# A four-layer cross-attention kernel: two single-precision products split in 16 bit parts, bias products on separate rows of the array, one shift and one exponential per GQA item, and a new order of the work

## The reference

```python
# GQA layer: 16 query heads of width 8, 4 key/value heads, no mask
xn = x * rsqrt(mean(x*x, -1) + 1e-5) * norm_w
q, k, v = xn @ wq, ctx @ wk, ctx @ wv
x = x + softmax(q k^T / sqrt(8)) v @ wo

# MHA layer: 16 heads of width 64
q, k, v = x @ Wq, ctx @ Wk, ctx @ Wv
logits = q k^T / 8 + col_bias        # -20*(1-mask[t]) in up to four key columns
x = x + softmax(logits) v @ Wo + bo
```

## Time and profile before

| | |
|---|---|
| median of three runs | 1851.74 us |
| profiled execution, its own time | 1852.7 us |
| its span, first to last instruction | 1850.9 us |
| PE / DVE / ACT / POOL busy, share of the span | 97% / 86% / 80% / 81% |
| mean granted TensorE clock | 0.977 of full speed |
| DMA | 320.36 MB, mean 173 GB/s |

### The profile page before, as it was taken

The page is one execution under the profiler, slowest core; times in us unless marked ns, Lnnn a source line. Parts: engine busy times, 40 slices in busy tenths (PEclk is TensorE's granted clock), DMA queues, the critical chain, the costliest instruction groups (busy, mean ns, idle before and its releaser), DMA issues.

```text
span 1850.9 us, 72762 instructions
## 1 busy us (share of the span) xinstructions
PE 1792.3 (97%) x28272; PEld 1557.7 (84%) x28272; DVE 1593.3 (86%) x3130; ACT 1471.6 (80%) x2859; POOL 1507.8 (81%) x1880
## 2 busy tenths in 40 slices
PE   6699999999999999999999999999999999999995
PEld 6578888888888888888888888888888888888884
DVE  6589988889888998898888998889888988889973
ACT  4378888888888888888888888888888888888872
POOL 3388888888888888888888888888888888888873
PEclk7599999999999999999999999999999999999998
DMA  5279999999999899999999999999899999989995
GB/s 170 42 140 183 167 187 183 184 182 166 178 192 180 181 168 184 185 173 188 175 180 187 177 175 178 182 190 177 176 178 186 185 173 177 169 176 178 177 165 128
DMA packets 1168210, 320.36 MB, mean 173 GB/s; under 512 B 1140246, under 2 KB 1164124, under 8 KB 1167868
## 3 DMA queue, kind: packets, MB, share of 16 engines
q1 hardware_dynamic: 1167868, 315.69, 93.1%
HBM read 15.93 MB, written 4.19 MB: 11 GB/s over the span
## 4 chain that ended last, share of the span: by engine, by line
PE 92%; issue 1%; DMA 0%; DVE 0%; POOL 0%; SPq 0%; ACT 0%
PE ring L1215 48%; PE sc L1352 11%; PE o_ps L1215 9%; PE o_ps L1370 5%; PE ring L1424 5%; PE sc L1335 4%; PE sc L1350 4%; PE ring L1286 2%; PE ring L1410 1%; PE ring L1405 1%; PE ring L1421 1%; PE sc L1327 1%; PE ring L1263 0%; PE o_ps L1366 0%; PE ring L1266 0%
## 5 line engine op out<-in xcount | busy, mean ns | idle before, releaser
L1215 PE MATMUL ring<-ctx_four,m_w 128*128 128x154 f16 x6144 | 441.4, 230 | 1.5 <-DVE v_tile L915 0.9
L1215 PEld LDWEIGHTS ring<-ctx_four,m_w 128*128 128x128 f16 x6144 | 422.8, 96 | 1.9 <-DVE v_tile L915 1.1
L636 POOL TENSOR_TENSOR p_sg<-arena,p_sg 128x512 f16<-128x512 f32 (+1 forms) x256 | 347.4, 1357 | 89.8 <-ACT p_sg L702 89.8
L1092 DVE TENSOR_TENSOR arena<-sc,row_max 128x616 f32<-128x616 f32 (+2 forms) x512 | 402.6, 797 | 13.2
L641 POOL TENSOR_TENSOR p_sm<-arena,p_sm 128x616 f16<-128x616 f32 x256 | 334.1, 1319 | 4.4 <-ACT p_sm L702 2.5
L664 POOL TENSOR_TENSOR arena<-arena 128x1024 f16<-128x1024 f32 x128 | 273.4, 2136 | 40.5 <-ACT arena L702 40.4
L702 ACT ACTIVATE arena<-ring 128x462 f16<-128x462 f32 (+1 forms) x384 | 198.3, 516 | 133.8 <-PE ring L1215 132.5
L1215 PE MATMUL ring<-wv_m,ctx_four 128*103 128x512 f16 (+1 forms) x1152 | 281.2, 380 | 0.6 <-DVE q_mix L919 0.6
L1071 DVE TENSOR_TENSOR arena<-ring,arena 128x462 f16<-128x462 f32 (+1 forms) x384 | 223.8, 584 | 64.2 <-ACT arena L702 55.4
L1352 PE MATMUL sc<-arena,x_s 128*128 128x512 f16 (+1 forms) x1152 | 262.2, 336 | 0.0
L1089 DVE TENSOR_REDUCE row_max<-sc 128x6 f32<-128x462 f32 (+2 forms) x384 | 223.7, 583 | 44.2 <-PE sc L1352 38.8
(11 more groups left out here) (165 smaller groups left out, 3797.4 us busy)
## 6 DMA issues: line engine op xcount, KB each, us to landing
v_fourth<-v_tile SPq DMA_DIRECT2D x64, 105.6 KB
ctx_nat<-in_ctx_dram SPq DMA_DIRECT2D x64, 77.0 KB
x_nat<-in_x_dram SPq DMA_DIRECT2D x64, 64.0 KB, 2.4
arena<-p_sg SPq DMA_TRANSPOSE x256, 3.9
arena<-p_sm SPq DMA_TRANSPOSE x256, 4.1
out_dram<-y_out SPq DMA_DIRECT2D x64, 64.0 KB, 2.1
v_fourth<-v_tile SPq DMA_DIRECT2D x32, 101.6 KB
arena<-in_L_xattn_Wk_dram SPq DMA_DIRECT2D x2, 1024.0 KB, 6.1
```

What stands on the lines that cost most here:

```text
L636: pool.tensor_tensor(p_sg[k][:, LO, 0:e - a], probs_flat[:, a:e], p_sg[k][:, HI, 0:e - a], ALU.subtract).then_inc(sems["pg_lo"], 1)
L1092: dve.tensor_tensor(shifted[:, hs, :], s_view[:, hs, :], row_max[:, hs].unsqueeze(2).to_broadcast([P, hs.stop - hs.start, S]), ALU.subtrac ...
L1215: ins = pe.matmul(out, a, b, start=(n == 0), stop=(n == len(passes) - 1))
```

## The change

- **Sum of squares.** POOL still squares `x` in f32 (`x_sq`, now two buffers). A new ACT step `squares` writes the square's high part in f16 straight from `x_f`, POOL subtracts it, and `scores_g` uses two f16 passes of one column against `ones_h`.
- **GQA output product.** `wo_g` is f16 high and low; `turned` makes two ACT copies (f16 high, f32), a new POOL step `low_turned` makes the low part, `output_g` has three f16 passes.
- **Bias products.** The six rows of `bias_l` and `bias_r` are copied to partitions 32 to 37 and 64 to 69 as well. `scores_m(m, 0)` issues the three bias products of all three banks at once, each with 6 rows from another group of 32 partitions, and waits for all of the shift before.
- **GQA shift and exponential** are one instruction each (1232 columns). GQA and MHA items have their own `shifted` and `probs` buffers, and the waits go to the item two before of the same kind.
- **Order.** On PE, `rest_and_turn` and the transpose stand at the start of the next pair, `output_m` comes behind the first folded chunk, `values_g` and `turn_inputs` go behind the scores of `m`, `output_g` stands between the first two `scores_m`. The whole lists of a pair are now:
  - PE: `rest_and_turn(g-4)`, `scores_g(g)`, folded 0, `output_m(m-6)`, folded 1 and 2, `keys_values(g+2)`, `scores_m(m,0)`, `output_g(g-4)`, `scores_m(m,1)`, `pick_values(g)`, `turn_inputs(g+4)`, `values_g(g-2)`, `queries(g+2)`, `scores_m(m,2)`, context values, `values_m(m-2)`, context values.
  - DVE: `maximum_g`, folded 0, `finish_m(m-6)`, `shift_g`, folded 1 and 2, `keys_values(g+2)`, `finish_g(g-4)`, `maximum_m` 0 and 1, `shift_m` 0, `normalise_g(g-2)`, `maximum_m` 2, `turn_context`, `shift_m` 1, `queries`, values, `normalise_m(m-2)` 0 and 1, values.
  - ACT: `turned(g-4)`, folded 0, `high_out(m-4)`, `last_layer(m-6)`, folded 1 and 2, `keys_values`, `exponential_g`, `high_g` 0 and 1, `first_x`, `picked_values`, `turn_context`, `queries`, `exponential_m` 0, values, `squares(g+4)`, `high_m` 0, `exponential_m` 1, values, `high_m` 1, `normalise_rest(m-2)`.
  - POOL: `pack_values(g-2)`, `inverse_norm(g)`, `low_turned(g-4)`, `low_out(m-4)`, `spread_keys(g+2)`, `x_parts(m+2)`, `low_part(g)` 0 and 1, `x_parts(g+4)`, `low_part(m)` 0 and 1.
- **Buffers.** The ring's order follows that of PE. `y_out` has four buffers for eight streams, with one more wait on ACT.

```diff
@@ ring_uses
-        return [("ym", m - 6, 0), ("g", lead, chunks[0]), ("g", lead, chunks[1]), ("g", lead, chunks[2]), ("kv", g + 2, 0),
-                *[("ct", g + 4, 0)] * (layer(g + 4) == 0 or n % PAIRS == CT_EXTRA), ("vp", g, 0), ("q", g + 2, 0), *[("v", j, k) for j, k in value_chunks(n)[0:1]], ("yg", g - 4, 0),
-                *[("v", j, k) for j, k in value_chunks(n)[1:2]], ("ot", g - 2, 0)]
+        return [("ot", g - 4, 0), ("g", lead, chunks[0]), ("ym", m - 6, 0), ("g", lead, chunks[1]), ("g", lead, chunks[2]),
+                ("kv", g + 2, 0), ("yg", g - 4, 0), ("vp", g, 0), *[("ct", g + 4, 0)] * (layer(g + 4) == 0 or n % PAIRS == CT_EXTRA), ("q", g + 2, 0),
+                *[("v", j, k) for j, k in value_chunks(n)[0:1]], *[("v", j, k) for j, k in value_chunks(n)[1:2]]]
@@ buffers
-        probs = in_arena(HS, F32).rearrange("p (h s) -> p h s", s=S)
-        shifted = in_arena(HS, F32).rearrange("p (h s) -> p h s", s=S)
+        probs_g, shifted_g = in_arena(HS, F32), in_arena(HS, F32)
+        probs_m, shifted_m = [in_arena(HS, F32).rearrange("p (h s) -> p h s", s=S) for n in range(2)]
@@ SP pair
-                if exists(it, m - 2) and part(m - 2) != 3:
-                    move_values(it, m - 2)
                 if exists(it, g):
                     turn_g(it, g, 0)
                     turn_g(it, g, 1)
+                if exists(it, m) and part(m) != 3:
+                    move_values(it, m)
@@ POOL x_parts, GQA items
-                    pool.tensor_tensor(x_sq[st][:, :], x_f[st][:, :], x_f[st][:, :], ALU.mult).then_inc(sems["sq"], 1)
+                    pool.tensor_tensor(sq[:, :], x_f[st][:, :], x_f[st][:, :], ALU.mult).then_inc(sems["sq_f32"], 1)
+                    pool.wait_ge(sems["sq_hi"], at("sq_hi", it, j, 1))
+                    pool.wait_ge(sems["sq_f32"], at("sq_f32", it, j, 1))
+                    pool.tensor_tensor(x_sp[st][:, LO, :], sq[:, :], x_sp[st][:, HI, :], ALU.subtract).then_inc(sems["sq"], 1)
@@ POOL
+            def low_turned(it, g):
+                pool.wait_ge(sems["ot_copy"], at("ot_copy", it, g, 1))
+                pool.tensor_tensor(o_tg[:, LO, :], o_tf[:, :], o_tg[:, HI, :], ALU.subtract).then_inc(sems["ot_lo"], 1)
@@ ACT
+            def squares(it, g):
+                st = stream(g)
+                act.wait_ge(sems["xg_f32"], at("xg_f32", it, g, 1))
+                act.activation(x_sp[st][:, HI, :], x_f[st][:, :], ACT.Square, scale=1.0).then_inc(sems["sq_hi"], 1)
...
+                act.activation(probs_g, shifted_g, ACT.Exp, bias=log_w[:, :], scale=rstd[:, r:r + 1]).then_inc(sems["pg_exp"], 1)
...
-                high(o_tg[:, :], ring[:, b, 0:T], 1.0).then_inc(sems["ot_copy"], 1)
+                high(o_tg[:, HI, :], ring[:, b, 0:T], 1.0).then_inc(sems["ot_hi"], 1)
+                high(o_tf[:, :], ring[:, b, 0:T], 1.0).then_inc(sems["ot_copy"], 1)
@@ DVE bias_factors, split_gqa_weights
+                for k in range(1, 3):
+                    step(dve.tensor_copy(bias_l[32 * k:32 * k + 6, :], bias_l[0:6, :]))
+                    for n in range(2):
+                        step(dve.tensor_copy(bias_r[n][32 * k:32 * k + 6, :, :], bias_r[n][0:6, :, :]))
+                    low(wo_g[n][:, LO], st_go[:, n, :], W_V, wo_g[n][:, HI]).then_inc(dve_ready, 1)
@@ DVE
-            def shift_g(it, g, k):
+            def shift_g(it, g):
                 dve.wait_ge(sems["sg_max"], at("sg_max", it, g, 1))
-                shifted_free(it, g, k)
-                shift(G_SUB[k], sems["sg_sub"])
+                if exists(it, g - 2):
+                    dve.wait_ge(sems["pg_exp"], at("pg_exp", it, g - 2, 1))
+                shift(shifted_g.rearrange("p (h s) -> p h s", s=S), slice(0, H), sems["sg_sub"])
@@ PE scores_g
-                pe.matmul(sc_flat[:, SS_COL:SS_COL + 1], x_sq[st][:, :], ones[:, :], start=True, stop=True)
+                for i in (HI, LO):
+                    pe.matmul(sc_flat[:, SS_COL:SS_COL + 1], x_sp[st][:, i, :], ones_h[:, :], start=(i == HI), stop=(i == LO))
@@ PE scores_m
-                scores_free(it, m, min(k, 1) + 1)
-                ind = bias_r[w][:, :, :].rearrange("p h s -> p (h s)")
                 a, e = k * BANK, min(HS, (k + 1) * BANK)
-                pe.matmul(sc_flat[:, a:e], bias_l[:, :], ind[:, a:e], start=True, stop=False)
+                if k == 0:
+                    scores_free(it, m, 2)
+                    ind = bias_r[w][:, :, :].rearrange("p h s -> p (h s)")
+                    for b in range(3):
+                        c0, c1, rows = b * BANK, min(HS, (b + 1) * BANK), slice(32 * b, 32 * b + 6)
+                        pe.matmul(sc_flat[:, c0:c1], bias_l[rows, :], ind[rows, c0:c1], start=True, stop=False)
@@ PE output_g
-                pe.matmul(ring[:, b, 0:T], wo_g[w][:, :], o_tg[:, :], start=True, stop=True).then_inc(sems["yg_raw"], 1)
+                split_product(ring[:, b, 0:T], [(hl(lambda i: wo_g[w][:, i, :]), hl(lambda i: o_tg[:, i, :]))]).then_inc(sems["yg_raw"], 1)
@@ PE pair
+                if exists(it, g - 4) or exists(it, m - 4):
+                    rest_and_turn(it, n, g - 4)
                 if exists(it, g):
                     scores_g(it, g)
```

More of the change, by code:

```diff
@@ L796, in queries, with exponential_g @@
                 high(q_hi[:, :, :], ring[:, b, :].rearrange("p (r t) -> p r t", t=T), 1.0).then_inc(sems["q_hi"], 1)
[L798 to L813, removed]
+            def exponential_g(it, g):
+                r = g // 2 % 2
+                act.wait_ge(sems["rstd"], at("rstd", it, g, 1))
+                act.wait_ge(sems["sg_sub"], at("sg_sub", it, g, 1))
+                if exists(it, g - 2):
+                    act.wait_ge(sems["pg_lo"], at("pg_lo", it, g - 2, 2))
+                act.activation(probs_g, shifted_g, ACT.Exp, bias=log_w[:, :], scale=rstd[:, r:r + 1]).then_inc(sems["pg_exp"], 1)
             def high_g(it, g, k):
                 a, e = G_COLS[k]
-                act.wait_ge(sems["pg_exp"], at("pg_exp", it, g, k + 1))
+                act.wait_ge(sems["pg_exp"], at("pg_exp", it, g, 1))
                 if exists(it, g - 2):
                     act.wait_ge(sems[f"turned_g{k}"], at(f"turned_g{k}", it, g - 2, 16))
-                high(p_sg[k][:, HI, 0:e - a], probs_flat[:, a:e], 1.0).then_inc(sems["pg_hi"], 1)
+                high(p_sg[k][:, HI, 0:e - a], probs_g[:, a:e], 1.0).then_inc(sems["pg_hi"], 1)
             def exponential_m(it, m, k):
@@ L825, in exponential_m @@
                 act.wait_ge(sems["sm_sub"], at("sm_sub", it, m, k + 1))
-                probs_free(it, m, k)
-                act.activation(probs[:, hs, :], shifted[:, hs, :], ACT.Exp, bias=log_w[:, :],
+                if exists(it, m - 2):
+                    act.wait_ge(sems["pm_lo"], at("pm_lo", it, m - 2, k + 1))
+                act.activation(probs_m[:, hs, :], shifted_m[:, hs, :], ACT.Exp, bias=log_w[:, :],
                                scale=MHA_SCALE).then_inc(sems["pm_exp"], 1)
@@ L883, in pair @@
                         values(it, n, j, k)
+                if exists(it, g + 4):
+                    squares(it, g + 4)
                 if exists(it, m):
-                    exponential_m(it, m, 0)
                     high_m(it, m, 0)
@@ L893, in pair @@
                 if exists(it, m - 2):
[L894 to L900, removed]
+                    normalise_rest(it, n + 1, m - 2)
             for n in range(-3, PAIRS):
@@ L1089, in maximum_m, with shift @@
                 dve.tensor_reduce(row_max[:, h0:h1], s_view[:, h0:h1, :], AX_X, ALU.max).then_inc(sems["sm_max"], 1)
-            def shift(hs, done):
-                dve.tensor_tensor(shifted[:, hs, :], s_view[:, hs, :], row_max[:, hs].unsqueeze(2).to_broadcast([P, hs.stop - hs.start, S]),
+            def shift(out, hs, done):
+                dve.tensor_tensor(out, s_view[:, hs, :], row_max[:, hs].unsqueeze(2).to_broadcast([P, hs.stop - hs.start, S]),
                                   ALU.subtract).then_inc(done, 1)
[L1095 to L1100, removed]
-            def shift_g(it, g, k):
+            def shift_g(it, g):
                 dve.wait_ge(sems["sg_max"], at("sg_max", it, g, 1))
-                shifted_free(it, g, k)
-                shift(G_SUB[k], sems["sg_sub"])
+                if exists(it, g - 2):
+                    dve.wait_ge(sems["pg_exp"], at("pg_exp", it, g - 2, 1))
+                shift(shifted_g.rearrange("p (h s) -> p h s", s=S), slice(0, H), sems["sg_sub"])
             def shift_m(it, m, k):
                 dve.wait_ge(sems["sm_max"], at("sm_max", it, m, k + 2))
-                shifted_free(it, m, k)
-                shift(slice(k * HALF, (k + 1) * HALF), sems["sm_sub"])
+                if exists(it, m - 2):
+                    dve.wait_ge(sems["pm_exp"], at("pm_exp", it, m - 2, k + 1))
+                hs = slice(k * HALF, (k + 1) * HALF)
+                shift(shifted_m[:, hs, :], hs, sems["sm_sub"])
             def normalise_g(it, g):
@@ L1160, in pair @@
                 lead, chunks = fold_work(n)
```

(17 more changed lines are left out.)

117 lines of the change are left out of this document (61 added, 56 removed).

## The result

The changed kernel takes 1820.74 us (median of four runs, 1819.92 to 1821.59) against 1851.98 (four runs, 1850.95 to 1853.34): ratio 0.9831, 95% interval 0.9814 to 0.9848. That is 31 us less, where 42 were forecast. The time lies in the forecast range (1800 to 1822), 1.3 us under its upper end. The profiled execution is the run of 1819.92, the fastest of the four, with a span of 1817.5, 33.4 us under the span before; so differences read from the two traces come out some 2 us larger than those of the medians.

The account below looks back on a forecast made before the run. PE, gapless from about 125 to 1809 us, was taken as the bound. From 1852.7 us, -0.36 us a pair times 125 (-45) and +3 for preparation gave 1810.7, forecast as 1810 us; range 1800 to 1822, chance 0.56.

Parts of the forecast that it names:

- The bound: PE is a gapless list from about 125 to 1809 us, so each 0.1 us per pair counts times 125 pairs.
- Squares and output product: PE passes for the sum of squares and GQA output: 0.09 and 0.05 us saved in each pair.
- Bias products: The three bias products on PE run side by side, 0.26 instead of 0.53 us: 0.27 saved in each pair.
- The overlap: Products on other rows of the array run at the same time, the second starting 0.04 us after the first.
- rows 5: Earlier trace's preparation: PE products of 64 rows changing once between halves of the rows, without a gap; starts 0.04 us apart.
- The change of rows: PE switching between 128-row and few-row products, into and out of the bias group: 0.05 us for both, possible 0 to 0.52.
- The second rival: Into and out of the bias group, each change waits 0.163 us for the pass before, 0.33 together: 1844 us; chance 0.12.
- the spacing of the pass before the group: Sign on PE: the pass before the bias group should be followed after its usual spacing.
- the first score pass: Sign on PE: starts 0.22 to 0.30 us after the first bias product; 0.4 or more means a change is paid for.
- Moves: Every other PE instruction is kept and only moved in the list; no gain or cost was put for it.
- the first rival: DVE comes to the shift 1 us later, so PE waits 0.2 us in each pair: 1835 us; chance 0.12.
- Before the first pair: Preparation: DVE's extra copies and low parts, which PE waits for, add 3 us, with 1.3 and 4.2 as ends.

## Why the prediction was right, and where it was off

The time fell into the range, and in part by luck. The steady stretch brought 18 us less than the sum had, mostly by one term that was mis-sized, and 8.6 us that were not in the sum came back from filling and emptying. Without these the kernel would have stood near 1829 us, outside the range.

**The bound.** Right: PE has 0.4 us or less of gaps in the steady stretch before and after, at full granted clock, and the steady saving is the saving of its list.

**Squares and output product.** Right: forecast 0.09 and 0.05 a pair, and 0.09 and 0.05 as means over the 121 pairs (0.08 and 0.05 in the rounded rows above). That is some 0.14 x 121 = 17 us, the larger part of the steady gain.

**Bias products.** The mechanism was right, in both halves, and the size of one term was off. The overlap was put too dear: group 0.26 from the 0.04 of the earlier trace rows, really about 0.22. The 0.04 was also misread: in rows 5 the pass into `ring` starts 0.17 after one pass into `sc` and 0.04 before the next, so it is the offset between two rows of products that run side by side, not the time from one start to the next; the three bias products start within 0.01 us of each other. The change of rows was put too cheap: "I take 0.05 for both", measured 0.20 in the group, 0.09 of it in and 0.10 out. Net saving of the bias group 0.09 to 0.10 (the run on all rows says 0.094) instead of 0.22; 0.12 x 121 = 15 us, more than the whole miss. The failure was one of choice: the range ran from 0 to 0.52, and the earlier trace rows, a change between two halves of the rows in products of one shape, was taken as the nearest row, though it shows no change of shape. The other argument for 0.05, that an uncovered weight load can't cost more than the 0.025 of a narrow pass, does not hold either: the profile gives the loads of these narrow passes 0.096 us each (L1386 of the changed kernel), so at 0.025 a pass they overlap each other and the passes, and their spacing prices no uncovered load. The second rival, which put the waits for the pass before at 0.163 each, erred by about as much on the other side: 0.33 for both, against 0.20 in the group and 0.18 with the extra product. The 0.09 to 0.10 each way is close to the length of one weight load; that the late load is the whole price is not shown.

Of the prediction's own signs, the spacing of the pass before the group (0.31 instead of its usual 0.22) was the one that told; the first score pass, 0.32 behind the group's start, fell between the 0.30 that was to mean right and the 0.40 that was to mean a price.

The Trainium skill (TensorEngine Tiling (Array Packing), Key Properties) says that a change of the tiling mode drains TensorE. The runs agree that it costs: 0.18 to 0.20 us there and back, with the next weights loaded late. That is less than the 0.163 each way which the second rival took for it from the profile's modelled ends.

**Moves.** Put at nothing. 0.225 us a pair was saved, and 0.09 + 0.05 + 0.10 was there to save. Taken unrounded the difference is 0.015 us, or just under 2 us in all (PE's 0.4 us of waiting among them); it lies in passes that were only moved.

**The other engines and the first rival.** Right that they don't pass PE. The bias group's margin behind the shift was 0.8 in the working; in the changed kernel the shift is over before the group in all 121 pairs, by 0.36 us at the least, 0.75 in the median and 1.40 at the most. The pair of the rows above is the one with the most, so it flatters. DVE's timeline there:

```profile
962.20 1.43 DVE L1099 TENSOR_REDUCE row_max<-sc 128x16 f32<-128x1232 f32 x1
963.64 0.64 DVE L1086 TENSOR_TENSOR arena<-ring,arena 128x462 f16<-128x462 f32 x1
964.19 1.43 DVE L1107 TENSOR_TENSOR arena<-sc,row_max 128x1232 f32<-128x1232 f32 x1
```

The shift ends at 965.6 and the group starts at 967.0. So the 0.8 was well judged, but a DVE only 0.4 us later would already have held up PE in the tightest pair. POOL's 93% (forecast 94%) cost nothing: PE's one listed wait in the stretch is the 0.4 us for transposed probabilities.

**Before the first pair.** Right: +3 forecast. DVE in the changed kernel:

```profile
43.82 0.18 DVE L1027 COPY bias_l<-bias_l 6x128 bf16<-6x128 bf16 x1
44.04 0.98 DVE L1029 COPY bias_r<-bias_r 6x1232 bf16<-6x1232 bf16 x2
```

A copy of 1232 columns takes 0.49 (0.5 was taken). The first transposed input starts at 57.8 instead of 55.3: +2.5.

**Filling and emptying.** Not in the sum. From 55 us to the score at 134.22 the new order wins 3.8 us (-1.3 with the 2.5 of preparation), and the end 4.8 us. The end can be read. ACT before, then after, in the last 30 us:

```profile
1837.79 0.28 ACT L702 ACTIVATE y_out<-ring 128x128 f32<-128x128 f32 x1 [5.17 <-PE ring L1424]
1837.96 1.05 ACT L702 ACTIVATE arena<-arena 128x1024 f16<-128x1024 f32 x1
```
```profile
1804.45 1.06 ACT L710 ACTIVATE arena<-arena 128x1024 f16<-128x1024 f32 x1
1806.74 0.28 ACT L710 ACTIVATE y_out<-ring 128x128 f32<-128x128 f32 x1 [1.24 <-PE ring L1440]
```

Before, the high part of the next result (`high_out`) stood behind the copy of the last output and so behind PE's output product of two items back. Now it goes first, and POOL's low part and the transpose start that much earlier. The last output products start 10.9 us apart before (1834.42, 1845.36 at L1421 of the kernel before) and 8.4 after (1803.38, 1811.80 at L1437). This is read from the order and the traces; it was not tested by a run of its own. Against it stands a loss: the prediction gave the transposes more time, but in the emptying PE waits longer for the transposed probabilities, 7.1 us over the whole span (0.4 of it in the steady stretch) where it was 2.9. PE's waits of the changed kernel, whole span, which answer to the earlier trace rows:

```profile
PE o_ps L1226 <- DMA arena<-p_sm: 7.1, 5, 2.5
PE ring L1437 <- issue: 6.7, 3, 5.1
```

The waits before the last output products fell from 16.1 to 6.7. Not all of the 8.6 us is the order's: up to 7 x 0.225 = 1.6 us are the shorter products in the seven pairs outside the stretch.

**The sum.** The steady stretch brought 27 us instead of 45. Of the difference 15 us is the bias group with its change of rows, just under 2 the moved passes, and the rest 4 pairs that I had counted as gapless beyond the stretch. Preparation came to 2.5 us for 3, and the 8.6 us of filling and emptying, which were not in the sum, made up for half of what the steady stretch lacked.

## What to carry to other kernels

Putting small products side by side on the rows of the array pays only against the price of going there and back, here 0.18 to 0.20 us each time: three products of 0.52 us became 0.22 and paid 0.20 back, and the one small product by itself lost 0.18. From this follows, though no run here tried it, that such a group should be filled, and that two groups should not be made of what fits in one. And where the bounds of a term (here 0 and 0.52) lie further apart than the miss one can afford, the row that its size is taken from has to show the same kind of event, not a similar picture. If none does, carry both bounds through the sum and let the range say so.

## What the hardware showed that I had not expected

- The way in is paid by the product ahead (0.31 us instead of 0.22 for six unchanged passes), with no wait in any list; the way out shows as a weight load that starts with its product instead of 0.09 us ahead of it, behind 0.22 us of idle time with "issue" as its releaser.
- Products on different groups of 32 rows start practically together: the three bias products of the changed kernel within 0.01 us, and they take 0.39 us to their modelled end, as one alone does.
- Six rows instead of 128 don't shorten a 512-column product: the second and third of the three on the same rows start 0.23 and 0.44 us behind the first, on all rows 0.22 and 0.43.
